# The first layer's slots laid out anew on all engines, and the row sums' reciprocals split and spread by two float32r products

## The reference, cut to what matters

```python
# small attention: bias on the query, one head
attn = softmax((x + embed[stage]) @ f.T);  y = attn @ f
# 16 heads with rotated q and k, causal mask, softmax over keys
q, k, v = split(y @ w_qkv.T + b_qkv);  q, k = rope(q, k)
probs = softmax(where(causal, q @ k.T / sqrt(16), -inf))
x = x + (probs @ v) @ w_out.T + b_out
# category: one 256 x 256 matrix per block
c = x @ W[cat] + b[cat]
# feed-forward on values rounded to a 4-bit float grid, 16 at a time
h = silu(quant(c) @ quant(w_gate).T) * (quant(c) @ quant(w_up).T)
x = x + quant(h) @ quant(w_down).T
```

## Time and profile before

| what | us |
|---|---|
| median of 3 runs | 2461.85 |
| the three runs | 2452.49, 2461.85, 2463.63 |
| the profiled execution, its own time | 2440.37 |
| its span, first to last instruction | 2438.6 |
| mean granted TensorE clock, share of full | 0.982 |

### The profile page before, as it was taken

One profiled execution on the slowest core, in us unless ns is written; L12 is line 12 of the kernel. 1 busy time (PEld: TensorE's weight loads), 2 busy tenths in 40 slices (PEclk: granted clock), 3 DMA queues, 4 the chain that ended last, 5 costly groups with the idle time before them and its releaser, 6 DMA issues.

```text
span 2438.6 us, 53844 instructions
## 1 busy us (share of the span) xinstructions
PE 2262.9 (93%) x18368; PEld 2057.9 (84%) x18368; DVE 1840.2 (75%) x5132; ACT 1291.7 (53%) x3839; POOL 1005.2 (41%) x1063
## 2 busy tenths in 40 slices
PE   4788989999887799999999999899999999999999
PEld 3677878778776688888888887799999999999999
DVE  5778787777878666666666665588868888888876
ACT  1666666666663455555555555434325555555522
POOL 5435445354444455555555554133322222222073
PEclk8999999999998899999999999899999999999999
DMA  4523323233240312212212113131226767777443
GB/s 138 177 87 102 107 88 109 86 99 107 82 129 3 82 38 56 51 44 56 50 45 57 47 47 85 28 79 36 45 73 226 233 229 234 237 230 236 146 121 124
DMA packets 196341, 259.23 MB, mean 106 GB/s; under 512 B 58646, under 2 KB 168486, under 8 KB 185318
## 3 DMA queue, kind: packets, MB, share of 16 engines
q1 hardware_dynamic: 187206, 237.13, 32.0%
q0 software_dynamic: 8864, 18.66, 3.0%
HBM read 176.10 MB, written 43.94 MB: 90 GB/s over the span
## 4 chain that ended last, share of the span: by engine, by line
PE 61%; DVE 15%; ACT 8%; POOL 7%; issue 6%; DMA 1%; POOLq 0%; SPq 0%; DVEq 0%; ACTq 0%
PE bank L55 51%; PE bank L136 6%; ACT Ph L654 2%; POOL P L1786 2%; ACT Ph L656 2%; PE bank L1296 1%; DVE Ph L815 1%; ACT PTh L666 1%; PE bank L1336 1%; DVE xe L921 1%; DVE sgs L945 1%; PE bank L399 1%; POOL Qn L1811 1%; POOL Qn L1809 1%; DVE hb L955 1%
## 5 line engine op out<-in xcount | busy, mean ns | idle before, releaser
L1490 ACT ACTIVATE P<-P,mx 128x144 f32<-128x144 f32 x512 | 206.2, 405 | 263.8 <-DVE mx L1611 262.9
L55 PE MATMUL bank<-xD_hi,w1e_lo 128*128 128x256 f32 x880 | 251.1, 285 | 0.0
L2623 POOL DMA_INDIRECT xE<-d_y,ixs x78 | 111.2, 1426 | 336.3 <-PE bank L136 300.8
L55 PE MATMUL bank<-w2e_hi,hrD_hi 128*128 128x256 f32 x880 | 249.0, 283 | 0.0
L55 PE MATMUL bank<-w2e_lo,hrD_hi 128*128 128x256 f32 x880 | 248.9, 283 | 0.0
L55 PE MATMUL bank<-w2e_hi,hrD_lo 128*128 128x256 f32 x880 | 248.9, 283 | 0.0
L1786 POOL TENSOR_TENSOR P<-P,rs 128x512 f32<-128x512 f32 x128 | 133.1, 1040 | 273.9 <-DVE rs L1620 270.4
L55 PE MATMUL bank<-xD_lo,w1e_hi 128*128 128x256 f32 x880 | 245.9, 279 | 0.0
L55 PE MATMUL bank<-xD_hi,w1e_hi 128*128 128x256 f32 x880 | 245.6, 279 | 0.0
L2232 ACT ACTIVATE hD<-bank,b1E 128x256 f32<-128x256 f32 x312 | 127.0, 473 | 197.2 <-PE bank L55 188.1
L1120 POOL TENSOR_TENSOR xe<-xe 128x704 f32<-128x704 f32 (+3 forms) x64 | 88.2, 1378 | 340.5 <-DVE xe L926 340.3
(11 more groups left out here) (324 smaller groups left out, 7922.3 us busy)
## 6 DMA issues: line engine op xcount, KB each, us to landing
w1raw<-in_ew SPq DMA_DIRECT2D x39, 1024.0 KB, 6.0
w2raw<-in_ew SPq DMA_DIRECT2D x39, 1024.0 KB, 4.9
stack<-d_rot SPq DMA_DIRECT2D x256, 96.0 KB, 2.7
K<-Kn SPq DMA_DIRECT2D x256, 72.0 KB, 2.1
d_rot<-QKh SPq DMA_DIRECT2D x64, 256.0 KB, 3.1
Q<-Qn SPq DMA_DIRECT2D x256, 64.0 KB, 2.0
d_ys<-oE SPq DMA_DIRECT2D x39, 256.0 KB, 2.6
d_rot<-QKl SPq DMA_DIRECT2D x32, 256.0 KB, 2.9
```

Of the source, the lines that this page charges most:

```text
L55: inst = e.matmul(out, l, r, start=k == 0, stop=k == len(pairs) - 1)
L1490: inst = e.activation(P1[t % 2][:, n, :], P1[t % 2][:, n, :], ACT.Exp, bias=mx1[t % 2][:, 2 * g + sg:2 * g + sg + 1], scale=-1.0, accum_ou ...
L2623: e.indirect_dma_start(out=xE[q % 2][c], out_offset=None, in_=d_y, in_offset=bass.IndirectOffsetOnAxis(ap=ixs[r % 4][:, c:c + 1].bitcast(U ...
```

## The change

All five programs are touched, all in the first layer. The reciprocals are no longer one float32 tile of 16 columns: DVE takes the reciprocal, copies it as float32r (high part) and subtracts to get the low part, both into a tile `rsp` of 128 columns that is cleared once. PE turns all 128 columns, ACT copies 128 rows as float32r, and two float32r products on 128 rows (the selector has ones for the high and the low row) spread them. On PE slot 0 has another order, and in slot 5 the category is turned ahead of the small attention's scores. On ACT copies of turned heads come ahead of the exponentials in slots 1 to 4, and the rounding of q and k goes from slots 1 and 3 to slots 3 and 4. On DVE the last two multiplications go from slot 0 to slot 7, in between the steps of the first hidden half, the inversion goes behind those, the second half's steps from slot 1 to slot 0, and the category's quantization ahead of the maxima in slot 4. On POOL the second half's rounding goes from slot 2 to slot 1, ahead of the rotation, and `heads_low` from slots 2 and 3 to slots 3 and 4.

```diff
+        rsp, sel0r = tile("rsp", 2, 128, dt=F32R), tile("sel0r", 2, 128, dt=F32R)
...
-                turn(e, [(banks[6][0:16, st * 128:st * 128 + 128], rs0[b % 2][:, st, :]) for st in range(2)]
+                turn(e, [(banks[6][:, st * 128:st * 128 + 128], rsp[:, st, :].bitcast(F32)) for st in range(2)]
...
-                    inst = e.matmul(halves(7)[:, G, :], sel0[0:16, G, :], rsT[0:16, :], start=True, stop=True)
+                    inst = e.matmul(halves(7)[:, G, :], sel0r[:, G, :], rsT, start=True, stop=True)
...
                     scores(P + 1)
+                    if p == 0:
+                        first_values(b + 1)
+                        turn_sums(b - 1)
                     if p % 2 == 0:
                         values(P // 2 - 1)
-                    if p == 0:
-                        turn_sums(b - 1)
-                        first_values(b + 1)
-                        spread_sums(b - 1)
...
                     turn_heads(P)
+                    if p == 0:
+                        spread_sums(b - 1)
...
                     if p == 5:
+                        turn_category(b - 1)
                         first_scores(b + 2)
-                        turn_category(b - 1)
...
-                e.activation(rsT[0:16, :], banks[6][0:16, 0:256], ACT.Copy).then_inc(c_rsT, 1)
+                e.activation(rsT, banks[6][:, 0:256], ACT.Copy).then_inc(c_rsT, 1)
...
+                e.activation(sel0r, sel0, ACT.Copy)
...
                         first_copy(b + 1)
+                        x1_high(b + 1)
                         sums_copy(b - 1)
-                        x1_high(b + 1)
...
+                    if 1 <= p <= 4:
+                        copy_turned(P)
+                    if p == 3:
+                        hidden_high(b - 2, 1)
                     exps(P + 1)
...
-                    copy_turned(P)
-                    if p == 1:
+                    if not 1 <= p <= 4:
+                        copy_turned(P)
+                    if p == (1 if b == -1 else 3):
                         heads_high(b + 1, 0)
-                    if p == 3:
+                    if p == (3 if b == -1 else 4):
                         heads_high(b + 1, 1)
...
-                e.reciprocal(rs0[b % 2], rs0[b % 2]).then_inc(v_ri, 1)
+                if b:
+                    e.wait_ge(p_rsT, b)
+                else:
+                    e.wait_ge(g_V, 2)
+                inv, hi, lo = rs0[b % 2], rsp[:, :, 0:16], rsp[:, :, 16:32]
+                e.reciprocal(inv, inv).then_inc(*vs.up())
+                e.wait_ge(s_v, vs.n)
+                e.tensor_copy(hi, inv).then_inc(*vs.up())
+                e.wait_ge(s_v, vs.n)
+                e.tensor_tensor(lo, inv, hi.bitcast(F32), ALU.subtract).then_inc(v_ri, 1)
...
-                    if p == 0:
-                        multiply(b - 2, 1, 0)
-                        multiply(b - 2, 1, 1)
...
                     if p == 6:
+                        category_low(b - 1)
                         first_max(b + 2)
-                        category_low(b - 1)
...
+                    if p == 4:
+                        category_quant(b - 1)
                     maxima(P + 1)
...
                     if p == 0:
                         hidden_scales(b - 2, 1)
-                        if b == B + 1:
-                            hidden_steps(b - 2, 1)
                         x1_low(b + 1)
+                        hidden_steps(b - 2, 1)
                     if p == 1:
                         turn_qk(b + 1, 0)
                         normal_out(b - 1)
-                        if b <= B:
-                            hidden_steps(b - 2, 1)
                         hidden_low(b - 2, 0)
...
                     if p == 3:
+                        hidden_low(b - 2, 1)
                         add_category(b - 1)
-                        hidden_low(b - 2, 1)
-                    if p == 4:
-                        category_quant(b - 1)
...
                         gated(b - 1, 1, 1)
+                        multiply(b - 1, 1, 0)
+                        hidden_steps(b - 1, 0, (0,))
+                        multiply(b - 1, 1, 1)
+                        hidden_steps(b - 1, 0, (1, 2))
                         invert_sums(b)
-                        hidden_steps(b - 1, 0)
...
+            e.memset(rsp.bitcast(F32), 0.0)
...
                         rounded(quant_of(b - 2, 1), 128, FFN)
-                    if p == 2 and 0 <= b - 2 < B:
+                    if p == 1 and 0 <= b - 2 < B:
                         rounded(quant_of(b - 2, 2), 128, FFN)
                     if p == 1:
                         rotate(b + 1, 0)
                     if p == 2:
                         rotate(b + 1, 1)
+                    if p == (2 if b == -1 else 3):
                         heads_low(b + 1, 0)
                     if p == 3 and b >= -1:
                         first_query(b + 2)
-                    if p == 3:
+                    if p == (3 if b == -1 else 4):
                         heads_low(b + 1, 1)
                     if p == 4 and 0 <= b - 1 < B:
                         rounded(quant_of(b - 1, 0), 128, 512)
```

More of the change, by code:

```diff
@@ L151, in program @@
         raw0 = folded(rots.rearrange("p a n -> p (a n)")[:, 0:1536], (2, 768))
-        w_out0, rsT, OT0 = tile("w_out0", 2, 256), tile("rsT", 256), tile("OT0", 2, 256)
+        w_out0, rsT, OT0 = tile("w_out0", 2, 256), tile("rsT", 256, dt=F32R), tile("OT0", 2, 256)
         sel0, Wc, bc, c2 = tile("sel0", 2, 128), tile("Wc", 2, 256), tile("bc", 256), tile("c2", 512)
@@ L311, in sync_ab @@
             load_in(0)
-            for dst, src in ((raw0, "w_qkv0"), (b_qk0, "b_qk0"), (rot0, "rot0k"), (sel0[0:16], "sel0"),
+            for dst, src in ((raw0, "w_qkv0"), (b_qk0, "b_qk0"), (rot0, "rot0k"), (sel0, "sel0"),
                              (w_out0, "w_out0"), (b_out0, "b_out0")):
@@ L776, in act_ab @@
                         hidden_high(b - 2, 0)
-                    if p == 3:
-                        hidden_high(b - 2, 1)
                     if p == 6:
@@ L913, in scales, with steps @@
                 e.reciprocal(rs, m).then_inc(*vs.up())
-            def steps(i, P, W, src):
+            def steps(i, P, W, src, parts=(0, 1, 2)):
                 nb = W // 16
@@ L919, in steps @@
                 x, s = xn[i % 2][0:P, 0:W], ex[i % 2][0:P, 0:W]
-                e.wait_ge(s_v, vs.n)
-                e.scalar_tensor_tensor(out=x.rearrange("p (n k) -> p n k", k=16), in0=src.rearrange("p (n k) -> p n k", k=16),
-                                       scalar=1.0 - 2.0 ** -23, in1=r3, op0=ALU.mult, op1=ALU.mult).then_inc(*vs.up())
-                e.wait_ge(s_v, vs.n)
-                e.tensor_scalar(s.bitcast(U32), x.bitcast(U32), 0x7F800000, None, ALU.bitwise_and).then_inc(*vs.up())
-                e.wait_ge(s_v, vs.n)
-                e.tensor_scalar(s, s, 1.0, MAGIC, ALU.max, ALU.mult).then_inc(v_st, 1)
+                if 0 in parts:
+                    e.wait_ge(s_v, vs.n)
+                    e.scalar_tensor_tensor(out=x.rearrange("p (n k) -> p n k", k=16),
+                                           in0=src.rearrange("p (n k) -> p n k", k=16),
+                                           scalar=1.0 - 2.0 ** -23, in1=r3, op0=ALU.mult, op1=ALU.mult).then_inc(*vs.up())
+                if 1 in parts:
+                    e.wait_ge(s_v, vs.n)
+                    e.tensor_scalar(s.bitcast(U32), x.bitcast(U32), 0x7F800000, None, ALU.bitwise_and).then_inc(*vs.up())
+                if 2 in parts:
+                    e.wait_ge(s_v, vs.n)
+                    e.tensor_scalar(s, s, 1.0, MAGIC, ALU.max, ALU.mult).then_inc(v_st, 1)
             def category_quant(b):
@@ L962, in hidden_scales, with hidden_steps @@
                 scales(quant_of(b, 1 + st), 128, FFN, hb[st])
-            def hidden_steps(b, st):
+            def hidden_steps(b, st, parts=(0, 1, 2)):
                 if not 0 <= b < B:
                     return
-                steps(quant_of(b, 1 + st), 128, FFN, hb[st])
+                steps(quant_of(b, 1 + st), 128, FFN, hb[st], parts)
             def hidden_low(b, st):
@@ L2725 @@
     A["w_out0"] = T2(np.ascontiguousarray(g["L0_attn_w_out"].T[rows]))
-    sel = np.zeros((16, 2, 128), np.float32)
+    sel = np.zeros((128, 2, 128), np.float32)
     for r in range(256):
-        sel[rows[r] // 16, r // 128, r % 128] = 1.0
+        sel[rows[r] // 16::16, r // 128, r % 128][0:2] = 1.0
     A["sel0"] = sel
```

## The result

The changed kernel takes 2571.93 us (median of four runs, 2568.18 to 2577.04) where the kernel before takes 2459.87 beside it: 1.0462 of it, 95% interval 1.0435 to 1.0489, so 112 us slower. The forecast was 2531 with a range up to 2558: the direction was right, the size too small by 41 us.

What follows compares the result with a forecast made beforehand. PE, busy 93% of the span, bounds the kernel. Block stretches 10.28 + 20.0 + 6.1 + 11.8 = 48.2 us against 43.27, 4.9 more in 14 passes, 69 us: 2531 us from a median of 2461.85, range 2452 to 2558.

Steps and rivals of the forecast that it cites:

- The two spread products: PE's products spreading the row sums: float32r instead of float32 saves 0.7 us of PE's work per block.
- the inversion: DVE's split reciprocal, delayed by POOL: ends 3.65 us after PE turned the next small softmax (bounds 2.4 and 5.35).
- The first projection: PE's projection waiting for DVE's x1_low: starts 7.95 us after PE turned the next small softmax, against 6.25 before.
- C to Q: From PE's finished category product to DVE's finished category quantization: 6.1 us against 6.02, two DVE steps waiting for POOL.
- Q to G: From DVE's finished category quantization to PE's first gate product: 11.8 us against 7.13, with 3.9 of idle PE.
- The first rival: Short DVE instructions and the quantization escape POOL: 0.9 us more per block, 2475 us in all; chance 0.16.
- the second: Faster: the queue closes up until PE alone sets it, block 41.4 us, 2435 us in all; chance 0.14.
- T to C: From PE having turned the next block's small softmax to its finished category product: 20.0 us against 19.84.
- third rival: New idle time lowers PE's clock, losing 1.7 us of work once a block: 2555 us in all; chance 0.20.
- main case: All priced waits occur, PE idling before the category's turn: block 48.2 us against 43.27, 2531 us in all; chance 0.50.
- two new waits of 0.4 and 0.6: Before PE's category product: scores wait 0.4 us for maxima, slot 3's turned heads 0.6 for exponentials behind a copy.
- 14 like passes: Passes b = 1 to 14, category beside next heads: each 4.9 us longer, 69 us in all.

Runs made afterwards that it cites:

- e3: The kernel before with the split products alone, all slots in their old places: 2477.66 us, ratio 1.0083.
- e4: The changed kernel with the split inversion moved ahead of the last multiplications and hidden steps on DVE: 2577.77 us, ratio 1.0487.
- e2: The changed kernel with the old row-sum products (one reciprocal, turn of 16 columns, two float32 products), new orders kept: 2574.47 us, ratio 1.0466.
- h2: The changed kernel with useless repeated scores' products on PE ahead of its 3.67 us wait for the category's rounding: 2550.38 us, ratio 1.0364.
- f2: The changed kernel with POOL rounding the category ahead of heads_low(1), and DVE writing normalized outputs one slot earlier: 2498.97 us, ratio 1.0162.
- e1: The changed kernel with one pair of POOL's steps swapped, the category's rounding ahead of heads_low(1): 2498.15 us, ratio 1.0159.
- h1: The changed kernel, split kept, with category rounding first and first query ahead of low heads on POOL, normalized outputs earlier on DVE: 2489.49 us, ratio 1.0109.
- f3: The changed kernel with old row-sum products, category rounding first and first query ahead of low heads on POOL, normalized outputs earlier: 2469.21 us, ratio 1.0033.
- f1: The changed kernel with the next block's first scores ahead of the category's turn on PE again: 2551.21 us, ratio 1.0362.

## Why the forecast was right and wrong

**Right, by its steps.** The two spread products take 0.48 with their drain, against 1.13: 0.65 off PE, forecast 0.7. DVE's copy waited for one POOL instruction and the subtraction slipped in before the next: the inversion ended at T + 3.7 (forecast 3.65). The first projection came at T + 7.82 (7.95), C to Q took 5.91 (6.1) with two steps stretched, Q to G 11.71 (11.8) with 3.67 of idle PE (3.9). The first rival (short instructions escape POOL) fell with the copy's 1.55, the second (PE alone sets it) with the 3.67. The rule of the Trainium skill (SBUF — State Buffer, "SBUF: two separate sides"), that DVE and GpSimd exclude each other from the ports they share, agrees with the copy: 1.55 here, and 0.18 for the same copy in e3 where POOL is idle. The forecast priced this wait at 1.6 per block. Less came back when the copy went: 0.4 of T to C at full clock in e4, where the next short instruction waits instead, and 1.1 in e2, which has no copy; neither run is faster.

**Wrong, the step that failed most: the clock.** The forecast put "the new idle time takes PE's clock down" as a third rival at 0.20, an alternative to the main case. It was no alternative: the main case itself forecast an idle stretch of 3.9 in each pass, and the row it quoted showed a clock of 0.60 behind one of 3.68. Against it stood the waits of up to 1.7 that left the clock at 1.00, a shorter idle time. h2 shows the cost: 18 us in the 13 blocks, 21.5 in the run. The rival's size, 1.7 per block, was near the measured 1.40.

**The term T to C**, forecast 20.0, measured 20.95. From the first projection to C the forecast took 13.6 less 1.7, because the wait for the turned probabilities goes, and added two new waits of 0.4 and 0.6. The old wait does go, and neither new one is in the trace; but in its place the same products wait 1.39 for DVE's normalized outputs, which free their bank; DVE writes them behind the next heads' rotation, late because the steps of the second half were moved ahead. f2 shows that wait gone by one move, and T to C 0.8 shorter by it. The whole term was 0.95 too small per block, 12 us in 13.

**The ends.** The forecast counted 14 like passes and nothing else: 4.9 for the pass ahead of the first whole block, which took 10.1, and nothing behind the blocks, where it took 6.0. That is 11 us.

**The sum of the miss**: in the 13 blocks 18 for the clock and 9 at full clock (634.45 of h2 less 561.44 is 73, the forecast 4.9 x 13 = 64), 11 at the ends. That is 38 of 43 us (112 less 69; the forecast started from a median 2 us higher, so 41 in absolute time); some 5 lie behind layer 1's start, where a difference of that size was not followed up.

**What one block's 7.01 consists of** (50.20 less 43.19): the rounding behind the low heads 3.89 (e1), the clock 1.40 (h2), T to C 1.11, and 0.7 that stays between Q and G in e1 (7.82 against 7.13), where the scores wait 1.2 for maxima that now come behind the quantization; C to Q gives 0.1 back. Of T to C the split is 0.9 to 1.1 (h1 against f3; e2 at full clock) and the normalized outputs 0.8 (f2); the two are not simply added, since the waits for the turned probabilities, 25.3 us in 12 blocks before, are gone from it.

The range ended at 2558 because the case with the clock was priced at 2555 with none of the main case's own bounds upon it: T to C alone was given a bound 0.7 above the value taken, some 10 us.

## What to carry to other kernels

When a change is expected to leave the engine that sets the time idle for some us in each pass, price the idle time and the work behind it at half clock together, where the trace holds a row of such a wait; it is not a separate case. In an engine's queue, put the instruction for which the busiest engine waits ahead of the one that itself waits for a third engine: moving two lines on POOL was worth 74 us. Work taken off the fullest engine pays only if its preparation doesn't fall on the engine that it waits for next: here 0.7 less on PE came with 0.9 more in the stretch (h1 against f3).

## What was not expected of the hardware

Useless products made a kernel faster: 2.8 us of them in each block, in an idle stretch of 3.67, took the run from 2571.93 to 2550.38, because the clock stayed at 1.00. Shorter waits can do the same harm: one of 2.09 (e3) was followed by the half clock in 5 of 13 blocks, one of 1.95 to 1.98 (f1) in 6 of 12, two of 0.38 and 1.38 close together (e2) in 10 of 13, while 1.65 alone (before) and 1.34 (f3) were never. So taking 1.1 us of waits out of a block (e2) could leave the run where it was. What decides between blocks with the same wait stays open. A copy of 32 columns on DVE took 0.18 or 1.55 us by what POOL was doing, and moving it out of POOL's way (e4) left the next short instruction to take 1.70.
